# One instruction of 1792 columns for both halves of a product's weights, on ScalarE and on GpSimd

## What is computed

```python
xn = _layernorm(x, axis=-1)
q = (xn @ Wq.T); k = (xn @ Wk.T); v = (xn @ Wv.T)      # split into heads of 128
q = _rmsnorm(q, q_norm_w); k = _rmsnorm(k, k_norm_w)
scores = jnp.einsum('bkgqd,bksd->bkgqs', qg, k) / math.sqrt(HD)
attn = jax.nn.softmax(scores + bias[None], axis=-1)    # ALiBi slopes, causal
s = einsum('bkgqs,bksd->bkgqd', attn, v) reshaped @ Wo.T
g = _silu(xn @ W.T + bias + lora_out)
x = x + s * g
```

## Time and profile before

| | us |
|---|---|
| median of 3 runs | 2917.84 |
| lowest, highest of the runs | 2912.51, 2919.3 |
| the profiled execution, its own time | 2914.61 |
| its span from first to last instruction | 2912.5 |
| TensorE busy in the span | 2641.0 |
| VectorE, ScalarE, GpSimd busy | 1739.6, 1751.4, 1700.2 |

### The profile page before, as it was taken

How to read it: one execution, slowest core, us unless ns; L and a number is a source line. 1 busy time by engine, 2 the same in 40 slices (tenths; PEclk the granted TensorE clock), 3 DMA queues, 4 the chain that set the end, 5 groups by cost and what they waited for, 6 DMA issues and landing times.

```text
span 2912.5 us, 39936 instructions
## 1 busy us (share of the span) xinstructions
PE 2641.0 (91%) x13840; PEld 2333.5 (80%) x13840; DVE 1739.6 (60%) x3556; ACT 1751.4 (60%) x4611; POOL 1700.2 (58%) x821
## 2 busy tenths in 40 slices
PE   3658887988989999999989999999999999999996
PEld 2547776877778788888878788888878888888885
DVE  5334565565676655565676655655666655555565
ACT  2235455545566566666756566667656666676663
POOL 3356565656566665655656756566556665665553
PEclk8879998998999999999999999999999999999999
DMA  7766565657434443333423443333423533333323
GB/s 253 241 227 221 191 220 206 234 185 241 176 112 129 146 130 114 109 121 114 134 93 103 164 129 109 116 115 107 145 89 100 179 116 114 114 105 121 114 71 119
DMA packets 184119, 424.48 MB, mean 146 GB/s; under 512 B 34544, under 2 KB 75632, under 8 KB 183024
## 3 DMA queue, kind: packets, MB, share of 16 engines
q1 hardware_dynamic: 183920, 421.93, 44.3%
HBM read 349.51 MB, written 89.13 MB: 151 GB/s over the span
## 4 chain that ended last, share of the span: by engine, by line
PE 78%; DVE 8%; POOL 4%; ACT 3%; DMA 3%; issue 2%; SPq 2%; POOLq 0%; DVEq 0%; ACTq 0%
PE proj L461 19%; PE proj L463 18%; PE proj L462 18%; PE tr L554 4%; PE sc L461 3%; PE sc L462 3%; PE sc L463 3%; PE ot L462 3%; PE ot L463 3%; PE tr L534 3%; PE ot L461 2%; POOL wl L884 1%; DMA wb_lo<-wo_in 1%; DVE xtok L1140 1%; DVE pT_lo L1060 1%
## 5 line engine op out<-in xcount | busy, mean ns | idle before, releaser
L884 POOL TENSOR_TENSOR wl<-wl,wh 128x896 fp32r<-128x896 f32 x448 | 989.6, 2237 | 700.2 <-ACT wh L680 700.1
L461 PE MATMUL proj<-wh,xh 128*128 128x448 f32 x1792 | 677.0, 378 | 56.7 <-POOL wl L884 44.2
L462 PE MATMUL proj<-wl,xh 128*128 128x448 f32 x1792 | 663.2, 370 | 0.0
L463 PE MATMUL proj<-wh,xl 128*128 128x448 f32 x1792 | 662.9, 370 | 0.0
L895 POOL TENSOR_TENSOR wb_lo<-wb_lo,wb_hi 128x1024 fp32r<-128x1024 f32 x128 | 306.5, 2395 | 398.5 <-ACT wb_hi L690 398.4
L747 ACT ACTIVATE prob<-prob,negmax 128x128 f32<-128x128 f32 (+3 forms) x512 | 286.7, 564 | 364.3 <-DVE negmax L1095 364.2
L1117 DVE TENSOR_TENSOR acc<-acc,proj 128x512 f32<-128x512 f32 x480 | 326.6, 682 | 222.4 <-PE proj L463 220.8
L680 ACT ACTIVATE wh<-wl 128x896 fp32r<-128x896 f32 x448 | 406.8, 966 | 71.2 <-DMA wl<-wu 70.5
L461 PE MATMUL proj<-o_hi,wb_hi 128*128 128x512 f32 x1024 | 430.2, 420 | 20.8 <-DVE acc L1117 14.2
L726 ACT ACTIVATE pT_hi<-tr 128x512 fp32r<-128x512 f32 (+3 forms) x512 | 197.1, 440 | 360.3 <-PE tr L554 360.1
L461 PEld LDWEIGHTS proj<-wh,xh 128*128 128x128 f32 x1792 | 340.9, 190 | 90.8 <-issue 44.8
(11 more groups left out here) (116 smaller groups left out, 4473.9 us busy)
## 6 DMA issues: line engine op xcount, KB each, us to landing
wl<-wu SPq DMA_DIRECT2D x448, 448.0 KB, 4.0
wb_lo<-wo_in SPq DMA_DIRECT2D x128, 512.0 KB, 3.3
wu<-xtok SPq DMA_DIRECT2D x98, 448.0 KB, 3.9
wo_in<-wo SPq DMA_DIRECT2D x32, 512.0 KB, 5.6
xtok<-wa SPq DMA_DIRECT2D x56, 256.0 KB, 4.8
gate_dram<-z_buf SPq DMA_DIRECT2D x32, 256.0 KB, 5.1
xtok<-xT SPq DMA_DIRECT2D x32, 256.0 KB, 4.8
xtok<-gate_dram SPq DMA_DIRECT2D x32, 256.0 KB, 5.3
```

The source lines that it names most:

```text
L461: pe.matmul(out, hi_l, hi_r, start=first, stop=False, skip_group_check=onto)
L462: pe.matmul(out, hi_l, lo_r, start=False, stop=False, skip_group_check=onto)
L463: return pe.matmul(out, lo_l, hi_r, start=False, stop=last, skip_group_check=onto)
L884: pool.tensor_tensor(w_slot(wl, w), w_slot(wl, w, True), w_slot(wh, w), ALU.subtract).then_inc(w_ready, 1)
```

## The change

ScalarE's rounding and GpSimd's subtraction take both halves of a product as one instruction on two neighbouring slots. ScalarE now waits for both loads before it starts; GpSimd waits for the one rounding, and both halves are told ready together (`w_ready` + 2). Loads, their waits and the matmuls stay. The helper for the whole product is `w_pair`.

```diff
+        def w_pair(t, w, f32=False):
+            ap = t[:, w % 4:w % 4 + 2].rearrange("p s k n -> p (s k n)")
             return ap.bitcast(F32) if f32 else ap
...
-            def split_w(w):
-                if w >= HW * NG:
+            def split_product(n, p):
+
+                if n >= NG:
                     return
+                w = HW * n + 2 * p
                 act.wait_ge(w_in[w % 4], 16 * (w // 4 + 1))
-                act.activation(w_slot(wh, w), w_slot(wl, w, True), ACT.Copy).then_inc(w_hi_done, 1)
-
-            def split_product(n, p):
-                for h in range(2):
-                    split_w(HW * n + 2 * p + h)
+                act.wait_ge(w_in[w % 4 + 1], 16 * (w // 4 + 1))
+                act.activation(w_pair(wh, w), w_pair(wl, w, True), ACT.Copy).then_inc(w_hi_done, 2)
...
-            def low_w(w):
-                if w >= HW * NG:
+            def low_product(n, p):
+                if n >= NG:
                     return
-                pool.wait_ge(w_hi_done, w + 1)
-                pool.tensor_tensor(w_slot(wl, w), w_slot(wl, w, True), w_slot(wh, w), ALU.subtract
-                                   ).then_inc(w_ready, 1)
-
-            def low_product(n, p):
-                for h in range(2):
-                    low_w(HW * n + 2 * p + h)
+                w = HW * n + 2 * p
+                pool.wait_ge(w_hi_done, w + 2)
+                pool.tensor_tensor(w_pair(wl, w), w_pair(wl, w, True), w_pair(wh, w), ALU.subtract
+                                   ).then_inc(w_ready, 2)
```

More of the change, by code:

```diff
@@ L228, in w_slot @@
             ap = t[:, w % 4].rearrange("p k n -> p (k n)")
+            return ap.bitcast(F32) if f32 else ap
+        def w_pair(t, w, f32=False):
+            ap = t[:, w % 4:w % 4 + 2].rearrange("p s k n -> p (s k n)")
             return ap.bitcast(F32) if f32 else ap
```

## The result

The changed kernel took 2970.28 us, the median of three runs (2968.99 to 2976.68), against 2917.84: the ratio is 1.0194, with an interval of 1.018 to 1.0209. The forecast was 2945, with a range of 2927 to 2965: slower, as forecast, but 52 us slower where the terms gave 28, and outside the range. The profiled execution took 2976.68 us, with a span of 2974.6 and a mean clock of 0.949.

What follows compares the result with a forecast made beforehand. TensorE bounds the kernel, busy throughout from round 6; late weights and VectorE's waits for GpSimd can move the time. Terms 7 + 6.6 - 6.4 + 5.7 + 7.5 + 5.7 + 2 = +28 us gave 2945, range 2927 to 2965.

Steps and rivals of the forecast that it cites:

- Term 1: Start and round 1's P1: TensorE gets its weights later, +7 us (4 to 10).
- Term 2: Weight sums, rounds 0 to 5: VectorE's sums end 1.1 us later, six times, +6.6 us (3 to 13).
- Rival (b): Weight sums: GpSimd's bias holds VectorE for all its 1.57 us, third sum 1.1 later, six times; 2952 us, chance 0.05.
- Term 5: Scaling of k, rounds 7, 15, 23: VectorE waits 2.5 us more for GpSimd; +7.5 us (0 to 9).
- Term 4: Gate's product, rounds 8, 16, 24: VectorE waits out 4.0 us, not 2.1; +5.7 us (0 to 7).
- Term 6: Other places at a change of batch, ln scaling and P2's weights: 1.9 us together, three times, +5.7 us (2 to 9).
- Term 3: Gate's product, rounds 0, 6, 14, 22: GpSimd starts later, so VectorE goes first; -6.4 us (-8 to 0).
- Term 7: P4 in every other round: weights about 0.05 us later, upper bounds 0.4; +2 us (0 to 14) including q0's delay.
- Term 8: q0 in every other round: L1050 waits for GpSimd's end; 0.05 us, upper bound 0.3; +2 (0 to 14) including P4's.

Runs made afterwards that it cites:

- 4: Changed kernel with ScalarE's pair kept, GpSimd subtracting in four instructions of 448 columns: 2937.51 us, ratio 1.0074 to the kernel before.
- kernel 11: Kernel before, GpSimd cut to 448 columns only where VectorE meets it, ScalarE's pair for P4 of rounds 7, 15, 23: 2893.29 us, ratio 0.992.
- 9: Changed kernel, but P6 and P7 of rounds 1 to 6 in halves on both engines: 2958.73 us, ratio 1.0149 to the kernel before.
- 10: Changed kernel, but P1, P2, P3 of rounds 8, 16, 24 and P4 of 9, 17, 25 in halves on both engines: 2941.95 us, ratio 1.0085.
- kernel 1: Changed kernel with ScalarE's pair kept, GpSimd subtracting in two halves as before: 2938.5 us, ratio 1.0082 to the kernel before.
- 6: Kernel before plus three reciprocals on VectorE ahead of k's scaling in rounds 7, 15 and 23: 2925.99 us, ratio 1.0039.
- 7: Kernel before plus four reciprocals on VectorE ahead of k's scaling in rounds 7, 15 and 23: 2926.88 us, ratio 1.0045.
- kernel 5: Kernel before, all in halves, but ScalarE waits for both loads ahead of the first half: 2922.41 us, ratio 1.0024.
- kernel 2: Changed kernel with GpSimd's pair kept, ScalarE rounding in halves as before: 2973.65 us, ratio 1.0199 to the kernel before.

## Why the prediction was wrong in size

- **The step that failed** is the price of a gap. Terms 2, 4 and 5 named VectorE's delay nearly to the tenth, and took as TensorE's loss its length alone; the runs show that the matmuls behind a longer gap run at a lower granted clock, which costs again (2.1 to 2.6 us at each k scaling, nearly as much as the delay). Beside that, two things had no term: the wait for both loads in the full rounds and in round 0, and VectorE's small instructions at a change of batch.
- **The mechanism** was right in the main: with more boundaries VectorE gets in sooner (kernels 4 and 11), and the places named, taken back one at a time, take back their loss (9 and 10). At the weight sums the later start of GpSimd makes 0.74 of the gap's 1.24 us (kernel 1); the prediction had both in its 1.1.
- **Term 1** came to its 7 by luck. Of that, 5 was put before the first score tile and 1.9 at round 1's P1. Measured: 7.3 before the tile; P1 came 1.8 later still, as forecast, but round 0's step 0 grew by 0.4 only. With starts that differ by up to 2.4 us unchanged, 5 against 7.3 is not told apart.
- **Term 2** named the gap (1.1 more, 1.24 measured), but priced the rounds by the gap alone: the steps 1 of rounds 0 to 5 grew by 10.7 us in place of 6.6, their gaps by 6.8. Rival (b) fell: two sums ran beside the bias, in 1.08 and 1.38 us.
- **Term 5** is the largest miss: 2.5 us a round forecast, 5.0 measured, of which the gap is 2.7 and the clock behind it 2.3 (kernels 6 and 7 against it). That is beyond its upper bound, 9 for the three. **Term 4**: VectorE's 1.9 more was right (1.95), but rounds 8, 16 and 24 grew by 2.9 each. The clock of 0.73 behind the gap was not measured apart.
- **Term 6** looked at P2's weights and at the layer norm's scaling (its gap grew by 0.9, 0.7 forecast). P2's matmul lost 0.6 us, and step 0 of rounds 7, 15 and 23 grew by 2.6: the term missed VectorE's little Newton steps there, the gate's L1121 behind them, and GpSimd's own sums, which TensorE waits for. It assumed that only wide rows of VectorE meet GpSimd; one of 8 columns meets it as well.
- **Term 3** held: the gate's product in rounds 0, 6, 14 and 22 took 0.68 us in place of some 2.5, and step 2 of the last three became 1.7 us shorter, as in kernel 11, which makes this move alone in these rounds. Step 1 became 1.1 shorter, too: L1029, which had started together with GpSimd's L895 and waited for it (2.94 us), came 0.2 us sooner than it and took 0.81. Two tenths decide who goes first there; in kernel 1 these steps kept their length.
- **Term 7** was too low: 0.05 forecast, 0.24 to 0.38 measured. ScalarE took 1.71 in place of 1.65, and GpSimd began 0.15 us after it and not 0.1. It lies near the upper end that the term gave. **Term 8** held in its price (0.05 a round, 0.06 measured), though L1050 for q0 took 2.97 us and not 2.4. The loads that came late (3.2 us) weren't in either: the diff's second wait on ScalarE was costed in none of these rounds, though `probs_hi` for the last key tile stands behind it in the queue.
- **Steps 2 and 3 of rounds 0 to 5**, +5.4 us where -1.6 was forecast: 2.3 are in step 2 of round 0, behind the wait for both loads. How much of it the wait makes was not measured apart: the step grew by 1.1 with the wait alone (kernel 5) and shrank by 1.2 with GpSimd's pair alone (kernel 2). Some 0.3 each are P4's; 1.6 in the steps 3 together stay open.
- **The range**: the terms' own bounds add up to +1 and +62, 2919 to 2980, and not to the 2925 to 2975 that the prediction gives. It left out values over 2965 because the terms would not all fall on one side. But what was missing, the clock behind each added gap, has the same sign in every term that adds one.

**The rule weighed**: that the port is held for a whole instruction (the Trainium skill, SBUF — State Buffer, Who interferes with whom) agrees with the rows of VectorE's two-input instructions against L888 shown here, down to the one of 8 columns with its 3.95 us, and not with those against the bias. L1121 and L1029, which read one tensor, waited for GpSimd's two-input L895 as well (2.60 and 2.94 us).

## What to carry to other kernels

Where GpSimd's two-input instructions meet VectorE's, the length of one instruction is how long VectorE may be held up: merging two of them saved 0.1 us and held VectorE up by as much as 4, cutting them further cost 0.15 us a cut. Kernel 11, with cuts only at the meetings and one product started later, gained 0.8%, some three quarters of it by the cuts. Price a new gap of TensorE by its length and, beside that, by the clock behind it, from a row where such a gap stands. And when two waits of an in-order engine move ahead of one instruction, read what is queued behind them for every place where the later transfer can be late.

## What the runs showed that was not expected

- Behind gaps of 2.70 us the granted clock over the next 7.2 us was 1.00, 0.79 and 0.76 in three like places of one execution, and 0.61, 0.57 and 0.64 behind gaps of 3.35 to 3.61 in the changed kernel; each place was at 1.00 before, and the changed kernel's was at 1.00 again from 952 us. A clock of 0.76 cost 1.4 to 1.5 us, one of 0.57 cost 2.6.
- A VectorE instruction of 8 columns took 3.95 us beside GpSimd's of 4.05, against 0.17 alone.
- ScalarE's copy of 1792 columns takes 1.715 us, where two of 896 took 1.81 and one 0.966: 0.1 us is saved by the merge, and the first half is there 0.75 us later.
